# Two-layer graph kernel, last gather group: PE's tile wait replaced by a table of the tiles that its jobs read

## The reference

```python
dst = dst[argsort(dst)]                       # edges come sorted by destination
# layer 1: agg = zeros_like(x).at[src].add(edge_attr)
# layer 2:
ht = relu(h @ W1 + b1)
msg = sigmoid(w * ht[src] + b_param)          # (100000, 256)
fsum = segment_sum(msg, dst, num_segments=6250)
c = (log(s / (1 - s)) - b_param) / w          # s = clip(fsum)
out = relu(bundle / norm(bundle))             # bundle = concat(ht, c) @ Wn + bn
```

## Time and profile before

| | us |
|---|---|
| median of 3 runs | 2949.75 (2943.0 to 2951.38) |
| the profiled execution | 2918.7, span 2917.0 |
| mean granted TensorE clock over the span | 0.836 of full speed |

### The profile page before, as it was taken

One profiled execution on the slowest core, in us unless ns is written; L12 is line 12 of the kernel. 1 busy time (PEld: TensorE's weight loads), 2 busy tenths in 40 slices (PEclk: granted clock), 3 DMA queues, 4 the chain that ended last, 5 costly groups with the idle time before them and its releaser, 6 DMA issues.

```text
span 2917.0 us, 36909 instructions
## 1 busy us (share of the span) xinstructions
PE 2107.8 (72%) x9923; PEld 1483.2 (51%) x9923; DVE 1824.2 (63%) x4995; ACT 1288.0 (44%) x4284; POOL 1787.9 (61%) x1714
## 2 busy tenths in 40 slices
PE   1569976677776877867997576777776777676785
PEld 0457754454554554545776354445455455443474
DVE  1574434665775775767775476677577677552586
ACT  0124443335444634635346343643553553463554
POOL 1577777767666666664025666666667667666337
PEclk9778886779887988988998687997888888885798
DMA  9888878435433333332546333333333333333143
GB/s 383 236 174 179 174 120 243 112 91 145 120 89 89 92 89 88 92 90 63 177 157 231 91 87 89 90 92 90 90 90 91 90 90 91 91 92 92 47 156 113
DMA packets 175359, 357.77 MB, mean 123 GB/s; under 512 B 32444, under 2 KB 100822, under 8 KB 172581
## 3 DMA queue, kind: packets, MB, share of 16 engines
q0 software_dynamic: 93168, 219.39, 30.0%
q1 hardware_dynamic: 70791, 101.03, 10.7%
q10 hardware_dynamic: 11200, 35.00, 3.2%
HBM read 275.21 MB, written 93.19 MB: 126 GB/s over the span
## 4 chain that ended last, share of the span: by engine, by line
PE 46%; DVE 23%; issue 12%; another core or an unknown queue 9%; SPq 3%; ACT 2%; DVEq 1%; POOL 1%; DMA 1%; POOLq 0%; ACTq 0%
PE bank L1405 44%; DVE agg L1171 11%; DVE oh L1103 3%; DVE hits L1099 3%; DVE store L1095 2%; SPq L452 1%; DVEq L1163 1%; ACT oh L791 1%; DVE cum L1056 1%; PE bank L1568 1%; SPq L480 1%; DVE store L904 1%; DVE cum L1063 1%; ACT store L719 0%
## 5 line engine op out<-in xcount | busy, mean ns | idle before, releaser
L1405 PE MATMUL bank<-store,oh 125*128 125x157 f16 (+2 forms) x6770 | 1530.0, 376 | 550.4 <-issue 213.4
L1405 PEld LDWEIGHTS bank<-store,oh 125*128 125x128 f16 (+1 forms) x6770 | 1012.9, 174 | 1003.4 <-issue 522.8
L1171 DVE TENSOR_TENSOR agg<-bank,agg 128x256 f32 x1845 | 777.4, 421 | 500.3 <-PE bank L1405 221.0
L646 POOL DMA_INDIRECT store<-g_table,idx_all x785 | 771.1, 982 | 386.1 <-issue 189.2
L791 ACT ACTIVATE oh<-dist 128x128 f32<-128x128 f32 x1845 | 499.1, 301 | 1079.4 <-PE bank L1405 610.9
L646 POOL DMA_INDIRECT store<-in_edge_attr,idx_all x628 | 626.1, 997 | 288.7 <-issue 144.8
L783 ACT ACTIVATE dist<-iota,nloc_all 128x128 f32<-128x128 f32 x1845 | 582.6, 386 | 74.0 <-DVE nloc_all L1143 38.2
L1095 DVE TENSOR_TENSOR store<-iota,ttab 125x628 f16<-125x628 f16 x360 | 173.4, 482 | 302.5 <-remote 210.6
L620 POOL DMA_INDIRECT agg_copy<-agg x160 | 251.8, 1574 | 173.5 <-ACT agg L746 79.4
L1103 DVE TENSOR_TENSOR oh<-hits,v 125x512 f16<-125x512 f16 x720 | 289.7, 422 | 6.4
L1405 PE MATMUL bank<-agg 128*128 128x256 f32 (+2 forms) x480 | 128.2, 419 | 55.3 <-DVE agg L1192 43.9
(11 more groups left out here) (207 smaller groups left out, 1512.1 us busy)
## 6 DMA issues: line engine op xcount, KB each, us to landing
agg_copy<-store ACTq DMA_DIRECT2D x4, 6400.0 KB
agg<-in_edge_attr SPq DMA_DIRECT2D x39, 512.0 KB, 4.3
store<-in_x SPq DMA_DIRECT2D x72, 256.0 KB
agg_copy<-agg_copy POOLq DMA_DIRECT2D x16, 800.0 KB
store<-g_table,idx_all POOLq DMA_INDIRECT x785
store<-in_edge_attr,idx_all POOLq DMA_INDIRECT x628
pre_scratch<-store SPq DMA_DIRECT2D x25, 256.0 KB
agg<-agg_copy SPq DMA_DIRECT2D x25, 256.0 KB
```

The costliest lines, as they stand in the source:

```text
L646: gp.indirect_dma_start(out=store[:, at % RING * D:(at % RING + 1) * D], out_offset=None, in_=table_dram, in_offset=bass.IndirectOffsetOnA ...
L1171: dve.tensor_tensor(to, pt[n % TB][:, 0:D], to, ALU.add).wait_op(s_mm, n + 1, "sem-ge").then_inc(s_acc, 1)
L1405: return pe.matmul(o, l, r, start=start, stop=stop, skip_group_check=skip)
```

## The change

For group 8 alone (`LASTG`), PE's tile wait changes. SP, which has nothing else to do then, waits for each beat of the group in order and counts the new semaphore `s_land` up by one (`forward`). From the job list, DVE computes 52 numbers into `need_all`: the tile that job 4k reads, divided by four, plus one, which is the count of beats that must have landed for it. PE loads them into registers, eight at a time, and before the jobs 4k - 3 to 4k (and before job 0) waits until `s_land` is at least that number (`hold`: a wait on a register and a NOP). POOL's guard against counting up `s_g` too early is now a wait on `s_land`; its wait for the job of step t - 16 is as it was.

`jobs_at` now hands out the 205 jobs of group 8 within its 157 steps: one a step up to step 48 (`LEAD`), then more, in ascending order, and no steps follow. The sequence of jobs that results is the same as before, since only group 8's own jobs are left from step 48 on, and no atoms stand between them.

```diff
+LEAD = 48
+NEEDS = -(-(JT - 1) // TB) + 1
...
+def hold(eng, sem, value):
+    eng.wait_ge(sem, value)
+    eng.nop(nofuse=True)
...
-            for t in range(TAILS):
-                yield STAGES[stage][-1] + 1, t
+            if STAGES[stage][-1] not in LASTG:
+                for t in range(TAILS):
+                    yield STAGES[stage][-1] + 1, t
+        LASTG = (SORTS - 1,)
+        def quick_jobs(t):
+            return t if t <= LEAD else LEAD + -(-(t - LEAD) * (JT - LEAD) // (TILES - LEAD))
...
-            if g in STAGES[stage]:
+            if g in LASTG:
+                jobs += [(g, p) for p in range(quick_jobs(t), quick_jobs(t + 1))]
+            elif g in STAGES[stage]:
                 jobs.append((g, t))
...
+            def forward(g):
+                for t in range(0, TILES, TB):
+                    sp.wait_ge(s_g[beat_of(g, t) % SLOTS], rows_landed(beat_of(g, t)))
+                    sp.sem_inc(s_land, 1)
...
-                        done = max(done, NTH[old // BEATS, old % BEATS * TB] + 1)
+                        if old // BEATS in LASTG:
+                            gp.wait_ge(s_land, landed_before(old // BEATS, old % BEATS * TB) + 1)
+                        else:
+                            done = max(done, NTH[old // BEATS, old % BEATS * TB] + 1)
...
+                    if sig in LASTG:
+                        dve.tensor_copy(need, jobtile[0:1, 0:JT:TB]).then_inc(s_need, 1)
+                        dve.wait_ge(s_need, 3 * last + 1)
+                        ts(need, need, TB.bit_length() - 1, None, ALU.logical_shift_right).then_inc(s_need, 1)
+                        dve.wait_ge(s_need, 3 * last + 2)
+                        ts(need, need, float(last * BEATS + 1), None, ALU.add).then_inc(s_need, 1)
...
+            def await_tiles(last, k):
+                at = last * NEEDS + k
+                if k % LOADS == 0:
+                    stop = (last + 1) * NEEDS if k + LOADS > NEEDS else at + LOADS
+                    _, values = nc.values_load_multi_w_load_instructions(
+                        need_all[0:1, at:stop], [mybir.EngineType.PE], min_val=1, max_val=BEATS)
+                    needs.update(((last, k + i), v) for i, v in enumerate(values))
+                hold(pe, s_land, needs.pop((last, k)))
...
-                        if p < TILES and p % TB == 0:
-                            beat = beat_of(g, p)
+                        if g_ in LASTG:
+                            if p % TB == min(p, 1):
+                                await_tiles(LASTG.index(g_), -(-p // TB))
+                        elif p < TILES and p % TB == 0:
+                            beat = beat_of(g_, p)
                             pe.wait_ge(s_g[beat % SLOTS], rows_landed(beat))
```

More of the change, by code:

```diff
@@ L172, in gnn_program @@
         lagr = sb("lagr", [1, JT], I32)
+        need_all = sb("need_all", [1, NEEDS], I32)
         code = sb("code", [P, TILES], F16)
@@ L318, in gnn_program @@
         s_abs, s_oh, s_mm, s_acc = (sem(n) for n in ("s_abs", "s_oh", "s_mm", "s_acc"))
+        s_land, s_need = sem("s_beatlanded"), sem("s_beatsneeded")
         s_rank, s_off = sem("s_rank"), sem("s_offsets")
@@ L407, in rows_landed, with landed_before @@
             return 16 * sum(TB if b % BEATS < BEATS - 1 else TILES - TB * (BEATS - 1) for b in range(beat % SLOTS, beat + 1, SLOTS))
+        def landed_before(g, t):
+            return LASTG.index(g) * BEATS + t // TB
         def load_starts(p):
@@ L563, in _ @@
                 column_starts(sig)
+            forward(LASTG[0])
             sp.wait_ge(s_mm, len(ORDER))
@@ L1128, in final_atom @@
                     ts(slot_all[:, sig % 2 * JW:sig % 2 * JW + JT], lagr[:, :], 8, None, ALU.logical_shift_left).then_inc(s_lag, 1)
+                    if sig in LASTG:
+                        last = LASTG.index(sig)
+                        need = need_all[:, last * NEEDS:(last + 1) * NEEDS]
+                        dve.tensor_copy(need, jobtile[0:1, 0:JT:TB]).then_inc(s_need, 1)
[3 more added lines that the diff above has]
+                        ts(need, need, float(last * BEATS + 1), None, ALU.add).then_inc(s_need, 1)
                 elif n == 4:
@@ L1177, in tiles @@
                     jobs, atoms = jobs_at(stage, g, t), atoms_at(stage, g, t)
-                    half = len(atoms) // 2 if len(jobs) == 2 else len(atoms)
+                    half = len(atoms) // 2 if len(jobs) >= 2 else len(atoms)
                     for a in atoms[:half]:
                         sort_atom(g + 1, a)
-                    add_job(*jobs[0])
+                    for job in jobs[:1]:
+                        add_job(*job)
                     for a in atoms[half:]:
                         sort_atom(g + 1, a)
-                    if len(jobs) == 2:
-                        add_job(*jobs[1])
+                    for job in jobs[1:]:
+                        add_job(*job)
             def find_same(b):
@@ L1652, in sum_job @@
                    ).wait_op(s_oh, n + 1, "sem-ge").then_inc(s_mm, 1)
+            def await_tiles(last, k):
[6 more added lines that the diff above has]
+                hold(pe, s_land, needs.pop((last, k)))
+            needs = {}
             def tiles(stage):
@@ L1657, in tiles @@
                         if p == 0:
-                            pe.wait_ge(s_off, g + 1)
-                        if p < TILES and p % TB == 0:
-                            beat = beat_of(g, p)
+                            pe.wait_ge(s_off, g_ + 1)
+                            if g_ in LASTG:
+                                pe.wait_ge(s_need, 3 * LASTG.index(g_) + 3)
+                        if g_ in LASTG:
+                            if p % TB == min(p, 1):
+                                await_tiles(LASTG.index(g_), -(-p // TB))
+                        elif p < TILES and p % TB == 0:
+                            beat = beat_of(g_, p)
                             pe.wait_ge(s_g[beat % SLOTS], rows_landed(beat))
```

## The result

| | before | after |
|---|---|---|
| median of 15 runs, us | 2945.28 (2938.57 to 2952.85) | 2954.74 (2948.50 to 2961.72) |
| ratio | | 1.0031, 95% interval 1.0021 to 1.0042 |
| span of the profiled execution, us | 2917.0 | 2955.3 |
| mean granted TensorE clock | 0.836 | 0.827 |

The changed kernel is 9.5 us slower, with an interval of 6.2 to 12.4 us. The two profiled spans differ by 38 us, and most of that says nothing of the change: the profiled execution of before (2918.7 us) was 27 us faster than the median of its kernel. The first gather of group 8 already comes 29 us later (2539.23 against 2509.97) behind eight groups in which the change does nothing. Only stretches within group 8 can be compared.

A forecast was written before the change was run, and what follows sets the result against it. Something between PE's start of a job and its end signal, not the tile wait, was taken to hold group 8's jobs while gathers run. Terms 0 + 0 + 1 + 0 + 1 = +2 us on 2917.0, plus 31 for the median: 2951, range 2910 to 2964.

The forecast's parts named there:

- The likeliest case: Group 8: easing PE's tile wait gains 0 us, small costs remain; +2 us, median 2951; chance 0.52.
- Step (3): DVE's three operations on 52 numbers, ahead of `idx_all` on POOL's path: about 1 us, bounds 0 and 1.4.
- Step (4): PE's register work, 52 holds and 7 table loads, two of them in the tails: 1 us, bounds 0 and 2.6.
- Rival one: Group 8: the tile wait ties jobs to steps, easing it frees them; 33 us less, 2917 or down to 2899; chance 0.22.
- Rival two: Register waits with NOPs stop PE's lookahead in group 8: +18 us, median 2968; chance 0.17 of over 9 us slower.

The follow-up runs named there:

- late case: Occasions on which the kernel before, unchanged, took 2918 to 2945 us; what decides the occasion is not known.
- prompt case: Occasions on which the kernel before, unchanged, took 2666 to 2673 us.
- both_waits: The kernel after, with PE also keeping the old tile wait beside the register waits; 2672.33 us against 2667.88 for the kernel before, ratio 1.0015.
- triple_after: The kernel after with PE's two MATMULs of a job done three times over for jobs 0 to 156 of group 8; 2944.73 us, ratio 1.0098 to the kernel before.
- triple_before: The kernel before with PE's two MATMULs of a job done three times over for jobs 0 to 156 of group 8; 2945.73 us, ratio 1.0103.
- half_holds: The kernel after with a register wait at every eighth job instead of every fourth; 2645.39 us, ratio 0.9923 to the kernel before.
- before_again: The kernel before, run again unchanged on another occasion; 2668.04 us, ratio 0.9997 against itself.
- Decoupled: The kernel before with group 8's gathers to one half of the ring and jobs reading one fixed tile in the other; three runs, 2640.37 to 2642.61 us.

## Why the prediction was right, and where only half

**The likeliest case.** I said +2 us and "the jobs don't move". In the late case, which both profiles were of, they don't: the change is 9.5 us slower, at the edge of what I called no change. The step that carried it, reading job 132's start and its addition 13 us later as "the tile wait is over", is confirmed by the DMA packets and by PE's starts: the beat of job 132 had landed 1.8 us before its bank was free, no beat of steps 52 to 156 was later than its bank, and the jobs with a tile wait start as soon as the others. (That POOL leads "by the full 16 tiles" elsewhere was too broad: at job 68 the beat was only 1.4 us ahead.) That profile and measurement both fell in the late case was luck. On a prompt occasion the same forecast, no change that can be told from none, would have missed a gain of 23 us.

**Its sizes.** Step (3), DVE's three operations: taken 1 us, measured 1.2 in the late case, hidden in the prompt one, where POOL goes on at 1.25 us through the start of group 8. Step (4), the register work: taken 1 us, bounds 0 and 2.6; the two loads in the tails cost 2.1 + 0.9 = 3.0 us in the late case and about 1.9 in the prompt one (both_waits: 1.6 ahead of job 157 and 0.3 further on). It was mis-sized because I took DVE's loads for PE's: DVE's load delays its additions by 0.34 us, whereas PE stood for 3.19 us at two loads in a row. That leaves some 5 us of the 9.5 unplaced. They may be the somewhat slower pace of jobs and gathers in steps 48 to 156, which a single pair of profiles can't prove. The tripled pair doesn't show it (triple_after / triple_before is 0.9997 by the medians).

**Rival one, the jobs run ahead.** It was given 0.22, and in the prompt case it is what happens: ratio 0.991, last addition 8 us behind the last gather, where the rival said 7. Its price, 33 us, was too high: the stretch behind the last gather shrinks by 35 - 8 = 27 us and the time by 23 (20 to 27). Its argument was that something ties jobs to steps. In the prompt case that is the tile wait, as PE's 45.7 us of idle time, the packets and the 23 us show. In the late case the results of PE come later than the tiles, and hide it. I argued against the rival from one row of one execution, which was sound for that occasion, and took it for a property of the kernel. Nothing in the profile of before alone would have told otherwise: all of its groups have their gathers at 1.42 to 1.49 us.

**Rival two, the holds.** The register waits don't stop PE: in the prompt case half of them made no difference (half_holds), and constants gave the same time as registers. For the late case the first profile after tells: in the tails the jobs 165 and 169, each with a register wait ahead of it, start 0.43 us behind the job before, less than the 0.69 us that a job takes from start to end.

**What stays open.** What makes PE's results late on some occasions is not known. It isn't the clock: in triple_before that is fully granted, and the results are late all the same. It isn't the transfers' own duration: the gathers' packets of 4 KB took 222 ns on average in steps 60 to 140 of group 8 in both cases. That gathers must be running is shown by the tails, which take 28.4 us in both. The traces differ in one more thing. Of `s_mm`'s 1845 updates the trace of before holds 1539, and of those of `s_rows0` 1120, while before_again has 1843 and 4596; the other traces of each case are alike in this. So updates are missing from the record on the occasions on which they come late: of the 108 of `s_mm` in steps 48 to 156 the trace of before has 89, in the tails nearly all. Whether the path of the signals, the recording of them or the chip is the cause, or these only go with it, no run here tells. Decoupled in the late case, and one chip measured on two occasions, would have been the next ones.

## What to carry to other kernels

Ask of a wait that you mean to ease what ends last ahead of the waiting instruction, and ask it on more than one occasion: the same kernel had its idle time at PE from landings on one and from late results on another, and the same change was worth -23 us and +9 us. Before you trust a view that names who ended a wait, see that the trace has that semaphore's updates; here the packets' own times had to decide. When work of a loop is packed more densely into steps, everything else that is tied to steps moves back. A register load ahead of the first instruction of a stretch that stands alone was on the path (DVE waited 2.65 us for it instead of 0.50); whether it would be hidden a few jobs earlier was not tried.

## What I had not expected of the hardware

The kernel before takes 2945 us on one occasion and 2668 on another, and 232 of 244 us between their two traces lie where indirect gathers run. In the late case PE's records show it working without a gap for 9.33 us while its results reach DVE up to 2.85 us apart and then five at once. In the prompt case a gather of 128 KB every 1.25 us (106 GB/s) doesn't slow PE, ACT or DVE at all.
